# Two graph convolutions on one core: loads and splits in halves at the start, the last tiles' row sums split differently, three groups first in the last stage

## The reference

```python
def _gcn_layer(x, adj, W, b):
    d_inv_sqrt = (jnp.sum(adj, axis=1) + 1e-09) ** (-0.5)
    msg = d_inv_sqrt[:, None] * adj * d_inv_sqrt[None, :] @ x
    return jax.nn.relu(msg @ W + b)
H_f = _gcn_layer(feature_x, adj, W_f, b_f)
H_s = _gcn_layer(spatial_x, adj, W_s, b_s)
attn = jax.nn.sigmoid(jnp.concatenate([H_f, H_s], axis=1) @ W_att + b_att)
out = _layernorm(x + attn * H_f + (1.0 - attn) * H_s, axis=-1)
```

## Time and profile before

| | us |
|---|---|
| median of 3 runs | 399.04 (397.78 to 402.72) |
| the profiled execution, its own time | 398.95 |
| its span, first to last instruction | 397.1 |
| TensorE busy (matmuls) | 373.2 |
| VectorE, ScalarE, GpSimd busy | 296.6, 284.6, 145.4 |
| moved by DMA | 132.86 MB |
| mean granted TensorE clock | 0.993 |

### The profile page before, as it was taken

How to read it: one execution, slowest core, us unless ns; L and a number is a source line. 1 busy time by engine, 2 the same in 40 slices (tenths; PEclk the granted TensorE clock), 3 DMA queues, 4 the chain that set the end, 5 groups by cost and what they waited for, 6 DMA issues and landing times. The chain is left out here.

```text
span 397.1 us, 5306 instructions
## 1 busy us (share of the span) xinstructions
PE 373.2 (94%) x1748; PEld 310.7 (78%) x1748; DVE 296.6 (75%) x417; ACT 284.6 (72%) x346; POOL 145.4 (37%) x189
## 2 busy tenths in 40 slices
PE   2997999999999999999999999999889999999991
PEld 2785786878888888888888888888668888888991
DVE  2768984968668793969397775919857797888896
ACT  3777788788878887777878887858492656578565
POOL 1000002571177226730459100002010417877765
PEclk9999999999999999999999999999999999999997
DMA  8999999999999999999999999999946534344011
GB/s 302 415 424 419 419 422 420 420 423 420 422 419 419 420 421 418 363 404 427 421 418 421 416 390 421 414 411 413 360 177 262 210 106 171 149 168 150 19 38 53
DMA packets 25371, 132.86 MB, mean 335 GB/s; under 512 B 2944, under 2 KB 7936, under 8 KB 11008
## 3 DMA queue, kind: packets, MB, share of 16 engines
q1 hardware_dynamic: 25344, 132.53, 82.7%
HBM read 130.42 MB, written 2.10 MB: 334 GB/s over the span
## 5 line engine op out<-in xcount | busy, mean ns | idle before, releaser
L380 PE MATMUL sums<-Ah,Yh 128*128 128x512 f32 (+1 forms) x528 | 204.0, 386 | 7.4 <-DVE Yl L482 4.1
L382 PE MATMUL sums<-Al,Yh 128*128 128x512 f32 (+1 forms) x528 | 202.2, 383 | 0.0
L381 PE MATMUL sums<-Ah,Yl 128*128 128x512 f32 (+1 forms) x528 | 202.2, 383 | 0.0
L471 DVE TENSOR_TENSOR Al<-raw,Ah 128x2048 fp32r<-128x2048 f32 (+1 forms) x70 | 153.6, 2201 | 35.3 <-ACT Ah L657 32.8
L657 ACT ACTIVATE Ah<-raw 128x2048 fp32r<-128x2048 f32 (+1 forms) x70 | 123.2, 1768 | 46.1 <-DMA raw<-in_At 32.3
L670 ACT ACTIVATE nat<-nat 128x2048 f32<-128x2048 f32 x54 | 103.6, 1918 | 28.4 <-DMA nat<-in_adj 27.2
L380 PEld LDWEIGHTS sums<-Ah,Yh 128*128 128x128 f32 x528 | 99.2, 188 | 30.4 <-DVE Yl L482 7.0
L382 PEld LDWEIGHTS sums<-Al,Yh 128*128 128x128 f32 x528 | 99.2, 188 | 19.6
L381 PEld LDWEIGHTS sums<-Ah,Yl 128*128 128x128 f32 x528 | 99.2, 188 | 18.9
L493 DVE TENSOR_TENSOR acc<-sums,acc 128x512 f32<-128x512 f32 (+1 forms) x122 | 77.5, 676 | 45.6 <-PE sums L382 45.6
L797 POOL TENSOR_TENSOR S<-S,raw 128x512 f32<-128x512 f32 x32 | 56.4, 1761 | 24.6 <-DMA raw<-in_At 21.8
(11 more groups left out here) (49 smaller groups left out, 139.0 us busy)
## 6 DMA issues: line engine op xcount, KB each, us to landing
raw<-in_At SPq DMA_DIRECT2D x64, 1024.0 KB, 9.3
nat<-in_adj SPq DMA_DIRECT2D x48, 1024.0 KB, 11.4
nat<-in_adj SPq DMA_DIRECT2D x8, 768.0 KB, 12.5
xs<-in_xs SPq DMA_DIRECT2D x7, 512.0 KB, 11.3
nat<-in_adj SPq DMA_DIRECT2D x8, 256.0 KB, 9.2
out<-xs SPq DMA_DIRECT2D x32, 64.0 KB, 1.9
xs<-in_xs SPq DMA_DIRECT2D x2, 128.0 KB, 6.8
xs<-in_xs SPq DMA_DIRECT2D x1, 256.0 KB, 11.6
```

The lines of the kernel that those rows point to most:

```text
L380: pe.matmul(to, Yh[:, t % YRING, hs], high, start=first, stop=False)
L381: pe.matmul(to, Yl[:, t % YRING, hs], high, start=False, stop=False)
L382: mm = pe.matmul(to, Yh[:, t % YRING, hs], low, start=False, stop=last)
L471: dve.tensor_tensor(Al[:, k % SPLITS, a * IB:b * IB], raw[:, k % RAWS, a * IB:b * IB], Ah[:, k % SPLITS, a * IB:b * IB], ALU.subtract).the ...
```

## The change

Items 0 to 19 are worked in pieces: item 0 as four blocks with its load in two DMAs, items 1 to 19 in two halves of 1024 columns for `high` and `low`, with `y_high` and `y_low` behind the first half, and TensorE waits for what each block needs instead of for the whole item. VectorE's evacuations in turns 0 to 19 stand ahead of, between and behind the halves. Part 1 of the row sums is loaded and summed in two halves; parts 4, 6 and 8 come one item later, beside 5, 7 and 9; parts 30 to 35 and most of 48 to 55 come one item earlier, as does the x load of tiles 16 to 19. GpSimd sums blocks of j-tiles 0 to 19 (8 blocks more, in items 1, 2, 5 and 6), so that the parts of tiles 24 to 31 are one DMA of 768 KB instead of two of 1 MB together, and are placed earlier. Group 2's item on tiles 24 to 27 comes before the items on tiles 28 to 31. W(3) is one item later. In turns 47 and 48 the evacuations come sooner. In the last stage `affine` stands ahead of `join`. The constants are loaded one item later. TensorE does 25 small matmuls ahead of the work, in three lots, instead of 10. At the very end GpSimd's and VectorE's last steps change places.

```diff
-PIECED = {0: 0, 2: 1}
-SHORT_TURNS = 8
-WARM = 10
+HALVED = 20
+WARM = [14, 8, 3]
 ...
-    order = [(0, s6), (1, s6), (0, s7), (1, s7)] + [(g, s) for g in range(2, G - 1) for s in (s6, s7)]
+    order = [(0, s6), (1, s6), (2, s6), (0, s7), (1, s7), (3, s6), (2, s7), (3, s7)]
+    order += [(g, s) for g in range(4, G - 1) for s in (s6, s7)]
 ...
-    SUMMED = range(GT, 5 * GT)
+    SUMMED = range(5 * GT)
+    PLAIN_FROM = len(SUMMED) * P
 ...
-    for n in range(4, 10):
-        parts[n - 1].append(n)
-    parts[9] = [10, 11]
-    for n in range(12, 36):
+    parts[4], parts[6], parts[8], parts[9] = [4, 5], [6, 7], [8, 9], [10, 11]
+    for n in range(12, 30):
         parts[n - 2].append(n)
-    for n in range(36, 2 * FULL):
+    for n in range(30, 2 * FULL):
         parts[n - 3].append(n)
-    for i, k in enumerate([45, 46, 46, 47, 48, 49, 49, 50]):
+    for i, k in enumerate([45, 45, 46, 46, 47, 48, 48, 49]):
 ...
+    SHARES = [(0, 0, N // 4), (1, 0, N // 8), (1, N // 4, N // 8)]
 ...
-        return max(whole, free) if r < FULL else max(whole, free, COLLECT + 4)
+        return max(whole, free) if r < FULL else whole + 1
 ...
-    BY_VECTOR = [T - 2, *HALVES[0], T - 1]
+    BY_VECTOR = [*HALVES[0], T - 2, T - 1]
 ...
+    def weigh_at(k):
+        return next((g for g in range(TAIL) if ends[g] + (2 if g == 3 else 1) == k), None)
 ...
+            if k == 0:
+                return [(i, i + 1) for i in range(GT)]
+            return [(0, 2), (2, GT)] if k < HALVED else [(0, GT)]
 ...
+                if k == 0:
+                    sp.dma_start(raw[:, 0, 0:2 * IB], At_v[0, :, 0:2 * IB]).then_inc(raw0_in[0], 16)
+                    sp.dma_start(raw[:, 0, 2 * IB:BLK], At_v[0, :, 2 * IB:BLK]).then_inc(raw0_in[1], 16)
 ...
+                if n == 1:
+                    sp.dma_start(nat[:, 1, 0:N // 4], adj_v[0, 1, :, 0:N // 4]).then_inc(nat1_first, 16)
+                    sp.dma_start(nat[:, 1, N // 4:N // 2], adj_v[0, 1, :, N // 4:N // 2]).then_inc(nat_in[1], 16)
 ...
-                    a, b = SUMMED[0] * P, (SUMMED[-1] + 1) * P
-                    sp.dma_start(nat[:, n % NATS, 0:a], adj_r[r, :, 0:a]).then_inc(nat_in[n % NATS], 16)
-                    sp.dma_start(nat[:, n % NATS, a:a + N - b], adj_r[r, :, b:N]).then_inc(nat_in[n % NATS], 16)
+                    sp.dma_start(nat[:, n % NATS, 0:N - PLAIN_FROM],
+                                 adj_r[r, :, PLAIN_FROM:N]).then_inc(nat_in[n % NATS], 16)
 ...
-            pe.wait_ge(pool_const, 7)
-            pe.wait_ge(rs_dve, 1)
-            for i in range(WARM):
-                pe.matmul(sums[:, 3, 1, 0:P], S[:, 0, 0:P], S[:, 0, 0:P], start=True, stop=True)
+            pe.wait_ge(pool_const, 8)
+            for n, count in enumerate(WARM):
+                if n >= 1:
+                    pe.wait_ge(rs_dve, n)
+                for i in range(count):
+                    pe.matmul(sums[:, 3, 1, 0:P], acc[:, 0, 0, 0:P], acc[:, 0, 0, 0:P],
+                              start=True, stop=True)
 ...
-                pe.wait_ge(Yl_ok, max(t for e, t in items[k]) + 1)
-                if k not in PIECED:
-                    pe.wait_ge(low_ok, GT * (k + 1))
-                due = group_at(k, 1)
+                due = weigh_at(k)
 ...
+                    if t + 1 > y_seen:
+                        y_seen = t + 1
+                        pe.wait_ge(Yl_ok, y_seen)
+                    split = GT * k + next(b for a, b in pieces(k) if j < b) if len(items[k]) == GT else GT * (k + 1)
+                    if split > low_seen:
+                        low_seen = split
+                        pe.wait_ge(low_ok, low_seen)
 ...
-                if len(ended) == GT:
-                    evacuate_new(ended[:3])
-                if len(ending) == GT:
-                    evacuate_new(ending[:1])
-                low(k)
-                if len(ending) == GT:
-                    evacuate_new(ending if k < SHORT_TURNS else ending[:2])
+                if k < HALVED:
+                    evacuate_new(ending[:2])
+                else:
+                    if len(ended) == GT:
+                        evacuate_new(ended[:3])
+                    if len(ending) == GT:
+                        evacuate_new(ending[:1])
+                for a, b in pieces(k):
+                    low(k, a, b)
+                    if a == 0:
+                        if k >= HALVED and len(ending) == GT:
+                            evacuate_new(ending[:2])
+                        if k in (FINAL - 1, FINAL):
+                            evacuate_new(ending[:1])
+                        for r in y_at[k]:
+                            y_low(r)
+                        if k < HALVED:
+                            evacuate_new(ending[:3])
+                if k < HALVED or k in (FINAL - 1, FINAL):
+                    evacuate_new(ending)
 ...
-                g = group_at(k, L_JOIN)
-                if g is not None:
-                    for r in of_group(g):
+                mixing, joining = group_at(k, L_MIX), group_at(k, L_JOIN)
+                if mixing is not None:
+                    for r in of_group(mixing):
+                        affine(r)
+                if joining is not None:
+                    for r in of_group(joining):
                         join(r)
-                g = group_at(k, L_MIX)
-                if g is not None:
-                    for r in of_group(g):
-                        affine(r)
-                    for r in of_group(g):
+                if mixing is not None:
+                    for r in of_group(mixing):
                         logit(r)
 ...
             mix(T - 1)
+            deviation(HALVES[0])
             last_deviation([T - 2])
-            deviation(HALVES[0])
             last_deviation([T - 1])
```

More of the change, by code:

```diff
@@ L310, in nat_here, with share_here @@
         def nat_here(eng, n):
-            pieces_in = sum(2 if m >= 2 * FULL else 1 for m in range(n % NATS, n + 1, NATS))
-            eng.wait_ge(nat_in[n % NATS], 16 * pieces_in)
+            eng.wait_ge(nat_in[n % NATS], 16 * (n // NATS + 1))
+        def share_here(eng, i):
+            eng.wait_ge(nat1_first if i == 1 else nat_in[SHARES[i][0]], 16)
         def part_summed(eng, n):
-            eng.wait_ge(rs_act, n + 1)
-            if n in SHARED:
-                eng.wait_ge(rs_dve, SHARED.index(n) + 1)
+            eng.wait_ge(rs_act, n + 1 if n < 1 else n + 2)
+            if n < 2:
+                eng.wait_ge(rs_dve, (1, 3)[n])
         @block.sync
@@ L443, in _ @@
                         weigh_half(HALVES[0])
-                    if k in PIECED and half == 0:
-                        pe.wait_ge(low_ok, GT * k + j + 1)
-                    e = items[k][j][0]
+                    e, t = items[k][j]
+                    if t + 1 > y_seen:
[5 more added lines that the diff above has]
+                        pe.wait_ge(low_ok, low_seen)
                     if e not in started:
@@ L464, in _, with low @@
         def _(dve):
-            def low(k):
+            def low(k, a, b):
                 if k >= SPLITS:
                     item_done(dve, k - SPLITS)
-                for a, b in pieces(k):
-                    raw_here(dve, k)
-                    dve.wait_ge(high_ok, GT * k + b)
-                    dve.tensor_tensor(Al[:, k % SPLITS, a * IB:b * IB], raw[:, k % RAWS, a * IB:b * IB],
-                                      Ah[:, k % SPLITS, a * IB:b * IB],
-                                      ALU.subtract).then_inc(low_ok, b - a)
-                    if k in PIECED and a == 0:
-                        y_low(PIECED[k])
+                raw_here(dve, k, a)
+                dve.wait_ge(high_ok, GT * k + b)
+                dve.tensor_tensor(Al[:, k % SPLITS, a * IB:b * IB], raw[:, k % RAWS, a * IB:b * IB],
+                                  Ah[:, k % SPLITS, a * IB:b * IB],
+                                  ALU.subtract).then_inc(low_ok, b - a)
             def y_low(r):
@@ L706, in of_group @@
                 return range(g * GT, (g + 1) * GT)
+            for i in range(3):
+                own_share(i)
             for k in range(K):
                 for n in parts[k]:
-                    row_sum(n)
+                    if n >= 2:
+                        row_sum(n)
                 high(k)
-                for r in y_at[k]:
-                    if r not in PIECED.values():
-                        y_high(r)
                 if k == FINAL + 4:
@@ L836, in _ @@
             pool.memset(share[:, :], -1.0 / F).then_inc(pool_const, 1)
-            pool.wait_ge(pool_const, 7)
+            pool.wait_ge(pool_const, 8)
             first_degree()
-            for k in range(2, FINAL):
+            for k in range(1, FINAL):
                 for r in range(1, FULL):
```

77 lines of the change are left out of this document (45 added, 32 removed).

## The result

| | us |
|---|---|
| forecast | 397.4 (range 393.0 to 400.8), faster than before |
| after, median of 20 | 398.5 (398.01 to 399.22) |
| before, median of 20 | 397.29 (396.66 to 402.72) |
| ratio after to before, 95% interval | 1.0027 (1.002 to 1.0035) |
| profiled execution after: time, span | 398.5, 396.7 |

The time is inside the range, and within 2%, but the change made the kernel 0.3% slower where I had it 0.4% faster. Two things have to be kept apart: what the change does, and what it is compared with. The profiled execution on which I built the sum took 398.95; the median of before over 20 executions is 397.29, so it was 1.7 above its own kernel's typical time (the three executions shown ahead, 397.78 to 402.72, all lay above it). The first experiment asks what was in it.

The account below looks back on a forecast made before the run. It took TensorE's unbroken matmuls as the bound from 95.2 to 247.4 us, with gains only ahead of, between and behind such stretches. 398.95 - 1.9 - 1.8 - 1.8 + 4.4 - 0.45 = 397.4; range 393.0 to 400.8.

Parts of the forecast that it names:

- ahead of item 50: TensorE's wait before item 50, behind part 55's late landing, goes because part 55 lands earlier: 1.8 us won.
- Items 47 to 51: Two TensorE stalls, within item 47 and before item 50, both go: 1.8 us won at each.
- start and items 1 to 13: Earlier first matmul and half-item splits bring item 14 forward: 1.9 us won, between 2.5 and 0.9.
- item 47: Its second run no longer waits for VectorE's late evacuation of a run of item 46: 1.8 us won.
- last stage: Group 0 ends an item later, so rounds and W(6) come late: 4.4 us lost, bounds 1 and 6.7.
- end: VectorE's last normalisations no longer wait for GpSimd's `rstd`: 0.45 us won, at least 0.
- the hard case: Items 1 to 13: GpSimd's block sums hold up VectorE; item 2 at 26.7, item 14 at 94.3, 0.9 us won.
- the free end: Items 1 to 13 without hindrance by block sums: item 14 at 92.7, 2.5 us won with the start.
- rival 3: Stalls at items 47 to 51 stay because the DMA queue sets item 48: 401.0, or 399.2 with half gone; chance 0.10.
- delays nothing: Last stage: W(3), one item later, starts at 43.5, before `affine` of group 3 at 45.9; no cost.
- Rival 1: The last stage catches up and costs only 1.0 us: 394.0; chance 0.30.
- rival 2: The last stage catches up nothing (6.7 lost), block sums take the start's gain, end wins nothing: 401.2; chance 0.15.

Follow-up runs that it names:

- The first experiment: The kernel before, profiled once more with no edit: 397.1 us, span 395.3.
- run 9: The kernel before with only the new row sums (GpSimd sums j-tiles 0 to 19, parts of tiles 24 to 31 one transfer each): 397.02 us, ratio 0.9994.
- run 10: The kernel before with the new row sums and the sooner evacuations of turns 47 and 48: 395.65 us, ratio 0.9966.
- run 2: The kernel after with the last stage's item order and the place of W(3) as in the kernel before: 394.43 us, ratio 0.9928 to before.
- run 15: run 2 with the old sequence of GpSimd's and VectorE's steps at the very end: 394.5 us, ratio 0.9933 to before.
- run 11: The kernel after, with GpSimd's block sums in items 2, 6, 11, 13 and 19 waiting for `y_low`: 399.98 us, ratio 1.0071 to before.
- run 8: The kernel before with only the evacuations of turns 47 and 48 made sooner: 397.01 us, ratio 1.0002.
- run 4: The kernel after with W(3) back behind item 56, the new item order kept: 399.15 us, ratio 1.0054 to before.
- runs 13: run 2 with items 3 to 19 split whole instead of in halves: 398.44 us, ratio 1.0035 to before.
- run 14: run 2 with items 3 to 19 split whole and VectorE's turns 3 to 19 as in the kernel before: 396.05 us, ratio 0.9959 to before.
- run 6: run 2 with `join` ahead of `affine`, as in the kernel before: 394.44 us, ratio 0.9914 to before.
- run 7: The kernel before with only the last stage's items in the new order, W(3) not moved: 402.0 us, ratio 1.0122.

## Why the prediction was wrong

**The failed step: the 1.8 won "ahead of item 50" (the second stall of the part "Items 47 to 51", and with it the base of 398.95).** A stall seen in one execution was counted as one of the kernel. In a second profile it is absent, and run 9, which makes part 55 early, has the time of the kernel before within 0.15%. Against 397.1, the execution without that stall, my own other terms give 397.1 - 1.9 - 1.8 + 4.4 - 0.45 = 397.35: the time as predicted, but no longer a gain, rather "no change". The forecast of a gain hung on that one term. That it became a loss is a second, smaller miss: the 1.15 between 397.35 and 398.5 are the sizes of the other terms, the start's above all. That the time came within 0.3% of the forecast is luck: the base was 1.7 too high and the sum of the terms 2.8 too low, and the two cancel but for 1.1. (The prediction took 2% for what a measurement can tell here; 20 executions of each kernel told 0.3%.)

**The other terms, in one view,** against the typical execution:

| term | forecast | measured | from |
|---|---|---|---|
| start and items 1 to 13 | -1.9 (-2.5 to -0.9) | -0.7 to -1.2 | item 14 in the table above; run 10 to run 2 |
| item 47 | -1.8 | -1.4 to -1.6 | runs 9 to 10; items 47 to 48 |
| ahead of item 50 | -1.8 | 0 | runs 1, 9 |
| last stage | +4.4 (1 to 6.7) | +3.7 to +4.1 | table; run 2 |
| end | -0.45 | 0 | run 15 |
| sum | -1.55 | +1.2 | medians of before and after |

**Start.** The mechanism was right and its size was that of the other end of my range. Item 2 was forecast at 25.1 freely and 26.7 in the hard case, and came at 26.28, with the block sums and `y_low` side by side as the earlier trace rows had shown; item 14 at 94.22 against the hard case's 94.3. What I argued for choosing nearer the free end ("item 9's landing forgives what item 2 loses") is true: run 11 moves item 2 by 0.9 and item 9 by 0.23. But the same holds for gains, so the 1.2 of the first matmul (0.7 in fact, 12.53; part 1's second half is summed from 9.41 and item 0's first half rounded from 10.64, 0.5 later than the 10.14 I had for its landing) could not be added either, and item 9 landed 0.65 later than in the trace of before. The halved load of part 1 brought nothing: its second half came 0.5 later than the whole part before, and D was ready at 11.27 instead of the forecast's 10.8 and before's 11.31. What is left of the term is the halves at item 9. The Trainium skill's page SBUF — State Buffer (section "Who interferes with whom"), cited in the prediction, says that such pairs exclude each other for the whole instruction; the 1.48 of `y_low` beside 3.50 of two sums agrees, and the term came out at its hard form.

**Items 47 and 50.** 1.6 within item 47 came true, but only because the row sums were changed with it. Runs 8 to 10 are the lesson: of two waits in a row on different engines, either can be removed for nothing as long as the other stays (ratios 1.0002 and 0.9994, with both gone 0.9966). In the typical execution part 55 lands just in time for a TensorE that the first wait has held up. I had counted both at their full idle time, as though each stood alone. In the kernel after both are really gone (51.46 busy of 51.5), so that rival 3 fell.

**Last stage.** It was right in mechanism and place and nearly in size (4.4 forecast, 3.7 to 4.1 measured). The first `join` was forecast to end 25.4 after item 51's start; it ended at 322.98, 25.36 after. Rounds forecast at 10.4, 12.7, 10.4, 12.1 were 10.3, 12.3, 10.3, 12.1 by the ends of the joins. W(6) was forecast 4.1 late and was 3.2 late against run 2; the first half of group 7 added 0.7. The forecast 0.6 of idle time ahead of W(4) didn't appear. Rival 1 (the cost shrinks to 1.0) and rival 2 (it is over 4.5) both fell: against run 2 it is 4.1. That W(3) "delays nothing" held: earlier, it stalls TensorE for 2.59, and the time is the same in one lot of run 4 and 1.4 longer in the other.

**End.** VectorE's two last normalisations have no wait, as forecast, but the four last stores are then issued one behind the other within 1.4 us, and run 15, which has the old end and its wait of 0.46 again, takes run 2's time. The span behind the last half-width matmul is 10.4 against 10.0 before; that is not the exchange, as run 15 has 10.4 with the old end and runs 13 and 14 have 9.9 with the new one.

What stays open: why part 55 landed 1.7 us later in the first profiled execution than in the second. The two traces show where they part. From the landing of item 44 to the sum of part 50 they agree within 0.1 us, and item 46's load is issued at 251.53 and 251.38; then ScalarE's `high` of item 46, in the first profile and in the second:

```profile
262.54 1.92 ACT L657 ACTIVATE Ah<-raw 128x2048 fp32r<-128x2048 f32 x1 [1.99 <-DMA raw<-in_At]
261.21 1.92 ACT L657 ACTIVATE Ah<-raw 128x2048 fp32r<-128x2048 f32 x1 [0.57 <-DMA raw<-in_At]
```

The 1.3 us between them stay in the queue (268.87 and 267.54 for item 47, 281.58 and 280.27 for item 49) until part 55, so whatever held up the landing of item 46 makes most of the 1.7. In run 8's profile `high` of item 46 starts at 262.66, also late. What holds it up, no trace shows.

## What to carry to other kernels

A stall that ends with a DMA landing should be looked for in a second execution before it is counted; the spread of the times hints at the need (396.66 to 398.72 for before and 396.69 to 397.43 for run 9, in which the part comes early, over 18 and 10 executions side by side). Where loads set the pace, gains and losses ahead of the next landing that TensorE waits for are both forgiven, so only what shortens the way from that landing to the matmul counts, and of two waits in a row both must go before either pays. In a pipeline of rounds that run at 12.04 us against a consumer's 12.7, an item that makes the first round start later costs nearly all of its lateness at the end, since each round can make up only the difference; order the work so that the first round starts as early as it can.

## What was unexpected of the hardware

In some executions TensorE's first matmuls ran at half pace in spite of the small matmuls ahead of them. The stretches 14 to 16 us of run 2 and of run 6, which have the same start:

```profile
14.00:16.00 2.00, 2.00 (x6) 1.52 (x6) 1.56 (x3) 1.48 (x2) 1.35 (x2) 0.50 0.99 422
```

```profile
14.00:16.00 2.00, 2.00 (x10) 1.62 (x10) 2.00 (x4) 1.48 (x2) 1.35 (x2) 1.00 1.02 434
```

The clock is 0.50 (1.2 GHz) with 6 matmuls against 1.00 (2.4 GHz) with 10; item 0 takes 7.20 against 5.79. Both start item 2 at 26.35, and the two executions took 394.58 and 394.44, so the lower clock costs nothing there, where item 2 is waited for anyway. It is not free everywhere: where the work behind it is without slack, as at W(3) in run 7, the time is lost, and the two lots of run 14 (395.3 at a mean clock of 0.992, 396.7 and more at 0.987 and less) and of run 4 go the same way. In the second profile of before item 0 took 7.28, its matmuls 0.427 apart, while the row of 14 to 16 us still gives the granted clock as 1.00:

```profile
14.00:16.00 2.00, 2.00 (x6) 1.54 (x6) 1.89 (x4) 2.00 (x2) 0.00 (x0) 1.00 1.00 422
```

There the distance of the starts tells more than the clock's column. Also, GpSimd's block sums stretched further than I had seen in the trace of before: a run of three took 8.14 us (2.7 each) in run 11, beside VectorE's splits and evacuations, where two took 4.83 (2.4 each) in the earlier trace rows.
